# Three transformer layers and a rotation on one core: the set-up reordered, clears moved to GpSimd

## The reference

```
mod = silu(cond) @ W_ada + b_ada           # shift, scale, gate, twice
h = layernorm(x) * (1 + scale1) + shift1
q, k, v = split(h @ W_qkv + b_qkv)          # 16 heads of 9
x = x + gate1 * (softmax(q k^T / 3) v @ W_proj + b_proj)
h = layernorm(x) * (1 + scale2) + shift2
x = x + gate2 * mlp(h)                      # 576 wide, gelu; layer 1: 4 experts, top 2
```

## Time and profile before

| | |
|---|---|
| median of 3 runs | 1291.34 us (1290.72 to 1295.43) |
| the profiled execution | 1287.96 us, of which span 1285.8 us |
| busy: PE, DVE, ACT, POOL | 1196.0, 908.0, 783.2, 744.0 us |
| chain that ended last | PE 79%, DVE 14%, issue 3%, ACT 1%, DMA 1% |
| PE busy in the 40 slices of 32 us | first slice 2 tenths, second 8, then 9 nearly throughout |
| granted PE clock in the same slices | 9, 6, 8 tenths, then mostly 9 |

### The profile page before, as it was taken

One profiled execution on the slowest core, in us unless ns is written; L12 is line 12 of the kernel. 1 busy time (PEld: TensorE's weight loads), 2 busy tenths in 40 slices (PEclk: granted clock), 3 DMA queues, 4 the chain that ended last, 5 costly groups with the idle time before them and its releaser, 6 DMA issues.

```text
span 1285.8 us, 35560 instructions
## 1 busy us (share of the span) xinstructions
PE 1196.0 (93%) x12842; PEld 957.8 (74%) x12842; DVE 908.0 (71%) x2505; ACT 783.2 (61%) x1801; POOL 744.0 (58%) x2221
## 2 busy tenths in 40 slices
PE   2899999989989999999998999999979999999997
PEld 1577777768767677778887888888767777777775
DVE  6689999866489999965664654646479999964432
ACT  2489888756479888962331432332468898864531
POOL 3665656566566665566667666677777777700000
PEclk9689999899989999999998999999979999989997
DMA  6322122332351112221110110110021111001120
GB/s 169 61 13 21 17 22 18 47 90 32 53 128 17 20 16 20 21 56 5 14 15 4 16 15 4 17 51 19 17 52 31 34 34 27 20 6 19 20 65 28
DMA packets 50320, 42.83 MB, mean 33 GB/s; under 512 B 8455, under 2 KB 45754, under 8 KB 49717
## 3 DMA queue, kind: packets, MB, share of 16 engines
q1 hardware_dynamic: 45884, 29.91, 10.4%
q0 software_dynamic: 3488, 8.52, 8.3%
q10 hardware_dynamic: 780, 2.17, 0.5%
HBM read 33.86 MB, written 3.03 MB: 29 GB/s over the span
## 4 chain that ended last, share of the span: by engine, by line
PE 79%; DVE 14%; issue 3%; ACT 1%; DMA 1%; SPq 0%; DVEq 0%; ACTq 0%
PE PS L1659 17%; PE PSA L1383 14%; PE PS L1464 7%; PE PSA L1440 7%; PE PS L1425 7%; PE PS L1383 6%; DVE BIG L547 3%; PE PS L1495 2%; PE PSB L1635 2%; PE PS L1485 2%; PE PS L1496 2%; PE PSB L1447 1%; PE PS L1490 1%; PE PS L1475 1%; PE PSB L1383 1%
## 5 line engine op out<-in xcount | busy, mean ns | idle before, releaser
L1245 ACT ACTIVATE BIG<-PSA 128x512 f32<-128x512 f32 (+1 forms) x224 | 132.0, 593 | 279.0 <-PE PSA L1383 278.8
L1659 PE MATMUL PS<-w,BIG 128*128 128x144 f32 (+1 forms) x1920 | 257.6, 289 | 9.7 <-DVE BIG L811 6.5
L1659 PEld LDWEIGHTS PS<-w,BIG 128*128 128x128 f32 (+1 forms) x1920 | 247.5, 191 | 18.1 <-DVE BIG L811 7.8
L547 DVE TENSOR_REDUCE BIG<-PSA 128x8 f32<-128x1024 f32 x192 | 234.2, 1220 | 33.2 <-PE PSA L1440 31.7
L1114 ACT ACTIVATE BIG<-PSB 128x1024 f32<-128x1024 f32 x192 | 195.6, 1019 | 19.6 <-PE PSB L1447 19.5
L1440 PEld LDWEIGHTS PSA<-KK,Q 32*128 32x128 f32 x1536 | 109.0, 195 | 63.3 <-issue 41.2
L1440 PE MATMUL PSA<-KK,Q 32*128 32x128 f32 x1536 | 134.0, 292 | 21.1 <-DVE BIG L547 10.7
L1425 PE MATMUL PS<-K,qt 128*128 128x128 f32 x768 | 125.0, 289 | 11.1 <-DVE qt L542 5.4
L1447 PE MATMUL PSB<-Q,KK 32*128 32x128 f32 x1536 | 133.3, 292 | 0.0
L1464 PE MATMUL PS<-BIG,VA 128*32 128x128 f32 x3072 | 127.6, 285 | 1.1 <-DVE col L422 1.1
L1856 POOL MEMSET qprod<- 128x2 f32 x63 | 6.3, 100 | 201.5 <-DMA VB<-QA 201.5
(11 more groups left out here) (302 smaller groups left out, 2977.6 us busy)
## 6 DMA issues: line engine op xcount, KB each, us to landing
gate<-gates SPq DMA_DIRECT2D x96, 72.0 KB, 2.9
mgate<-gates SPq DMA_DIRECT2D x96, 72.0 KB, 2.8
VB<-skew POOLq DMA_DIRECT2D x16, 288.0 KB, 3.7
X<-in_x SPq DMA_DIRECT2D x4, 576.0 KB, 14.0
out<-X SPq DMA_DIRECT2D x8, 288.0 KB, 3.6
BIG<-in_skew_w SPq DMA_DIRECT2D x2, 1024.0 KB
w<-in_w SPq DMA_DIRECT2D x1, 1440.0 KB, 11.4
BIG<-in_wqkv SPq DMA_DIRECT2D x2, 584.0 KB
```

The source lines that it names most:

```text
L547: V.tensor_reduce(nmax.rearrange("p (s w) -> p s w", w=HP)[:, 2 * a:2 * a + 2, 3 * HD:3 * HD + G], PSA[:, :].rearrange("p (r g k) -> p r g ...
L1245: S.activation(hm[0:rows, slot, :], PS[(par * FTOT[l] + j) % 2][0:rows, :], gelu).then_inc(gelu_done, 1)
L1659: last = mm(o, hm[0:rows, slot, s * 128:(s + 1) * 128], w2[0:rows, FT * e + k, :], start=(k == 0), stop=(k == FT - 1))
```

## The change

Five edits, all in the set-up:

1. SP: the first quarter of `x` is issued ahead of layer 0's column weights, not behind them.
2. ACT: the copies of the column products and of `QA` (with the waits that they need) come ahead of the issues of the gate weights and of the column weights of layers 1 and 2.
3. DVE gives the clears of `h3`, `qt` and `VA` and their ones to POOL, which does them between its constants and its first broadcast. The semaphores follow: `h3_set` (DVE waits for it before its first low part), `qt_set`, `va_zero` (ACT and PE).
4. DVE: `constant_parts` comes first, ahead of the first statistics.
5. DVE: the second quarter's statistics are taken inside `pair(-1)`, after `h_second(0)`, not before it.

```diff
 # sync
+            load_x(0)
             sp.dma_start(AC0[0], d["ada_col"][0:C0, 0:AC]).then_inc(ld_ada0, 16)
             load_rows(sp, AC1[0], d["ada_col"][:, 0:AC], ld_ada0)
...
-            for q in range(4):
+            for q in range(1, 4):
                 load_x(q)
 # vector
-            V.memset(h3[:, :, :].bitcast(F32), 0.0)
-            V.memset(qt[:, :, :, :, :].bitcast(F32), 0.0).then_inc(qt_set, 1)
-            dve.wait_ge(qt_set, 1)
-            for g in range(G):
-                last = V.memset(qt[:, :, 1, HG * g:HG * g + HG, 3 * HD + g:3 * HD + g + 1].bitcast(F32), 1.0)
-            last.then_inc(qt_set, 1)
...
-                def pair(i, dev=None):
+                def pair(i, dev=None, stats=None):
...
                     if 0 <= i + 1 < NL:
                         h_second(i + 1)
+                    if stats:
+                        first_stats(stats)
                     step(1)
...
                 if l == 0:
+                    constant_parts()
                     first_stats(0)
                     columns(0, PS[1])
                     deviations(0, 0, 0)
                     pair(-2)
                     qkv_split(0)
-                    values_clear(1)
-                    constant_parts()
-                    first_stats(1)
-                    pair(-1)
+                    dve.wait_ge(h3_set, 1)
+                    pair(-1, stats=1)
 # scalar: the nine issues of ada_gate and of ada_col for l in (1, 2) go from
 # ahead of act.wait_ge(s_const, 2) to behind the copy of QA
...
-                        act.wait_ge(va_set, (1, 1, 3)[l])
+                        act.wait_ge(va_zero, 1) if l < 2 else act.wait_ge(va_set, 2)
 # tensor
-                        pe.wait_ge(va_set, 2 + 2 * (l // 2))
+                        pe.wait_ge(va_zero, 2)
+                        pe.wait_ge(va_set, 1 if l < 2 else 3)
 # gpsimd, behind the tensor_scalar that writes UT
+            R.memset(h3[:, :, :].bitcast(F32), 0.0).then_inc(h3_set, 1)
+            R.memset(qt[:, :, :, :, :].bitcast(F32), 0.0).then_inc(qt_set, 1)
+            R.memset(VA[:, :, :, :], 0.0).then_inc(va_zero, 1)
+            pool.wait_ge(qt_set, 1)
+            for g in range(G):
+                last = R.memset(qt[:, :, 1, HG * g:HG * g + HG, 3 * HD + g:3 * HD + g + 1].bitcast(F32), 1.0)
+            last.then_inc(qt_set, 1)
+            pool.wait_ge(va_zero, 1)
+            for j in range(2):
+                at = j * (HD + 1) + HD
+                last = R.memset(VA[:, :, 8 * j:8 * j + 8, at:at + 1], 1.0)
+            last.then_inc(va_zero, 1)
```

More of the change, by code:

```diff
@@ L181, in program @@
         qkv_ps, qk_hi, qk_lo, v_ev, va_set = (sem("qkv_product"), sem("qk_high"), sem("qk_low"), sem("v_ready"), sem("va_set"))
+        h3_set, va_zero = sem("h3_set"), sem("values_cleared")
         qk_turn, qk_rd, qk_dup, qt_set = sem("qk_turned"), sem("qk_ready"), sem("qk_doubled"), sem("qt_set")
@@ L270, in _ @@
             sp.dma_start(K[:, :], d["consts"]).then_inc(ld_cond, 16)
-            sp.dma_start(AC0[0], d["ada_col"][0:C0, 0:AC]).then_inc(ld_ada0, 16)
-            load_rows(sp, AC1[0], d["ada_col"][:, 0:AC], ld_ada0)
             def load_x(q):
@@ L277, in load_x @@
                              d["x"][q * 8:(q + 1) * 8].rearrange("b t c -> t b c")).then_inc(ld_x[q], 16)
+            load_x(0)
+            sp.dma_start(AC0[0], d["ada_col"][0:C0, 0:AC]).then_inc(ld_ada0, 16)
+            load_rows(sp, AC1[0], d["ada_col"][:, 0:AC], ld_ada0)
             def load_raw(name, n, s):
@@ L405, in constant_parts, with values_clear @@
                 V.memset(oq[:, :, C:C + 1], 1.0).then_inc(va_set, 1)
-            def values_clear(n):
+            def values_clear():
                 V.memset(VA[:, :, :, :], 0.0).then_inc(va_set, 1)
-                dve.wait_ge(va_set, n)
+                dve.wait_ge(va_set, 2)
                 for j in range(2):
@@ L879, in mlp_step @@
                     if m == 6:
-                        values_clear(3)
+                        values_clear()
                     if not last:
@@ L1008, in _ @@
                 load_rows(act, wr3[k * C1:(k + 1) * C1, :], d["wqkv0"], ld_wq)
[L1009 to L1012, removed]
-                load_rows(act, AC1[l], d["ada_col"][:, l * AC:(l + 1) * AC], ld_ada)
             act.wait_ge(s_const, 2)
@@ L1022, in _ @@
             S.activation(QA[:, :], PS[6][:, 0:C], ACT.Copy).then_inc(q_at, 1)
+            act.dma_start(AG0, d["ada_gate"][0:C0, :]).then_inc(ld_gw, 16)
+            load_rows(act, AG1, d["ada_gate"], ld_gw)
+            for l in (1, 2):
+                act.dma_start(AC0[l], d["ada_col"][0:C0, l * AC:(l + 1) * AC]).then_inc(ld_ada, 16)
+                load_rows(act, AC1[l], d["ada_col"][:, l * AC:(l + 1) * AC], ld_ada)
             def mlp_cast(l, q):
```

## The result

The changed kernel took 1275.32 us (median of 4 executions, 1265.83 to 1281.95). The kernel before took 1291.03 us beside it (4 executions, 1289.20 to 1295.43). The ratio on record is 0.9891, 95% interval 0.9848 to 0.9935; it is not the quotient of the two medians, which is 0.9878. Its profiled execution took 1275.29 us (span 1273.0); the one of before took 1287.96 (span 1285.8). The later experiments, with more executions of both kernels, put the difference at 6 to 7 us of the mean: 1286.2 for the kernel before (85 later executions), and 1279.5 for the changed one (28, the first four among them) or 1280.3 (24, without them). Three of all these executions, each over 1.5% above the fastest of its kernel, are left out of the ratios and kept in the means.

A forecast was written before the change was run, and what follows sets the result against it. It took the set-up chain (x's transfer, then DVE's unbroken work until PE's first qkv product at 27.98 us) as the bound; 2.9 + 2.45 + 0.5 = 5.85, say 5.8, off the 1291.34 median gave 1285.5, range 1280.0 to 1291.0.

The forecast's parts named there:

- medians move by a few us: Whole time: the scatter allowed for medians when judging the chance of being faster by over 0.5%, put at 0.44.
- Part 1: Set-up loads: first quarter of x ahead, columns later; columns copied at 12.7 instead of 15.62, gain 2.9 us.
- they start at 6.0 and share: SP's queue: column weights start at 6.0 us beside ACT's qkv weights, landing taken as 9.9.
- A: Column weights land late, 10.45 us after issue, at 13.0; gain only 2.8 us, time 1288.5; chance 0.12.
- B: Column weights take 15.1 us, landing at 17.7; loss of 1.9 us, time 1293.2; chance 0.05.
- Part 2: DVE: nothing left between the weights' split and the low parts, which wait for ACT's high parts; gain 2.45 us.
- Part 3: Clears on POOL: 5120 columns, over between 9.0 and 16.0 us, taken as 10.5; cost 0.
- Part 4: DVE's steps after the columns run before POOL's first two-input instruction; gain 0.5 us, from 0 to 0.9.
- POOL's clears read no data and stand beside DVE's idle time: Set-up: the reason why DVE's gain from a quiet POOL could not go below 0.
- Rival C: PE's clock helps: denser start changes one pair, 3.6 us more, 1281.9; against it, PE's row-maximum wait remains; chance 0.15.
- D: PE's clock hurts: one pair more at the low level, 3.6 us lost, time 1289.1; chance 0.09.
- E: Does nothing: another engine takes the gain back before the end, time 1291; chance 0.03.

The follow-up runs named there:

- loads' order: Kernel before with only the first quarter of x issued ahead of the column weights: 1283.49 us, ratio 0.9992.
- ACT's copies: Kernel before with only ACT's copies moved ahead of its nine later issues: 1279.83 us, ratio 0.9991.
- clears, statistics: Changed kernel with the load order and ACT's copies taken back, leaving clears on POOL, constants first, statistics moved: 1286.2 us, ratio 1.0024.
- changed, delayed: Changed kernel with five further clears of MW3 on DVE ahead of the first low part: 1285.4 us, ratio 0.9978.
- before, clock kept up: Kernel before with 104 added identity products on PE, placed in its three waits: 1294.07 us, ratio 1.0043.
- wait away: Changed kernel with MW3's clear and the last sixteen statistics moved into DVE's idle time inside pair(-1): 1274.62 us, ratio 0.9892; repeated, 1276.49 us, 0.9924.
- wait away, clock kept up: Changed kernel with MW3's clear and last sixteen statistics inside pair(-1), plus 26 identity products in PE's three waits: 1273.51 us, ratio 0.9919.
- better version: Changed kernel with MW3's clear and last sixteen statistics inside pair(-1), and POOL's clears held until silu is done: 1271.83 us, ratio 0.9868.
- the pair of traces above: Two repeat runs of the changed kernel, no edit: 1281.69 us, ratio 0.9936, and 1281.81 us, ratio 0.9942; their traces' spans were 1280.7 and 1268.8 us.
- the third trace of the same kernel: Changed kernel run a third time, no edit, against the kernel before: 1281.81 us, ratio 0.9942.

## Why the prediction missed

Two steps failed. In the sum, it is the load order, 1.2 us short. In the time, it is "medians move by a few us": the sum goes from the 1291.34 of before to a median of the changed kernel as if only the set-up lay between them, and puts the scatter of executions at nothing in the forecast and at a few us in the range. The runs showed a gain of 7.54 us at the product, 6 to 7 at the end, and executions of one and the same kernel 20 us apart, which is where the rest of the 16 is most likely from.

**All executions together.** Call lost clock (1 - the mean granted clock) times the span. Over 195 executions of these kernels, a level for each kernel plus one slope leaves a scatter of 3.3 us. The slope is 0.47 us for each microsecond lost (0.43 within the kernel before alone). The earlier trace rows say the same: a pair at the low level takes 3.6 us more and loses 7.9 (half of 15.8), which is 0.46. The kernel before lost 17.9 to 55.6 us of clock in its executions and took 1275.7 to 1295.7.

| kernel | product | executions, mean | at no lost clock, against before |
|---|---|---|---|
| before | 27.98 | 85, 1286.2 | 0 |
| loads' order | 23.38 | 10, 1281.8 | -5.2 |
| ACT's copies | 25.89 | 10, 1280.2 | -2.7 |
| clears, statistics | 24.38 | 10, 1284.8 | -2.0 |
| changed | 20.07 to 20.44 | 28, 1279.5 | -6.4 |
| changed, delayed | 30.42 | 12, 1285.9 | +2.1 |
| before, clock kept up | 35.95 | 12, 1293.5 | +4.4 |
| wait away | 20.28, 20.70 | 15, 1275.5 | -8.9 |
| wait away, clock kept up | 19.68 | 6, 1274.3 | -13.9 |
| better version | 20.60 | 6, 1271.6 | -10.6 |

A value of 10 executions is good to about 1 us (one standard error). The last column follows the first, roughly: 7.5 us at the product are 6.4 at the end, and 2.4 us of delay are 2.1. It has a weakness that the pair of traces above shows: before the first recorded fall the record says 1.00 whatever PE's level is, so a kernel that rises and falls early has a loss on record that a kernel low from the start has not. This flatters the kernel with the wait away and the clock kept up: its mean is 1.2 us below that of the kernel without the added products, and this column says 5.0. The executions ran on three chips; the kernel before, at no lost clock, stands within 1.6 us on all of them.

Where the clock is lost is much the same in every trace: in all fourteen of them the recorded clock falls between 340 and 380 us, between 900 and 960, and in the last 40 us. No edit here touches those stretches.

**Part 1, the load order: right in kind, 1.2 us short, for a wrong reason.** The failed step is "they start at 6.0 and share". The working took ACT's delay for SP's queue: q1's first bytes moved about 1 us after the first issue (0.74 and 1.75), not 1.9, and x and the weights were through on q1 before ACT's q10, with its first issue at 4.20, moved a byte. `x` landed at 6.7 (issued at 2.13, and 4.6 more; forecast 7.5) and PE started on the weights at 8.63, not 9.9: just below the 8.8 that I had called undisturbed. The columns were copied 4.09 earlier instead of 2.9. The statistics, forecast "near 7.5", started at 9.29, because DVE was still at silu and the constant parts; they were over 0.46 us before the columns came, so this cost nothing. Rivals A and B, on late weights, fell: 5.9 us from their first issue to the last landing (2.61 to 8.49), not 10.45 or 15.1. (B's break-even, given as a landing at 16.1, is 15.8 by the working's own terms.)
**Part 2, nothing before the low parts: right.** PE's turn to the low parts took 5.88 and takes 3.51: 2.37, forecast 2.45. ACT released them, and the statistics were hidden.

**Part 3, clears on POOL: right at the fast end.** 0.9 ns a column and over at 9.4 with the small ones (forecast 10.5); PE had no wait for `U`.

**Part 4, DVE beside POOL: the gain was there, its lower bound was wrong.** From the columns' copy to PE's turn of the first pair took 5.40 and takes 4.47: 0.93 (forecast 0.5, and 0.9 was the upper end), as POOL's first two-input instruction came only at 17.54. But "POOL's clears read no data and stand beside DVE's idle time" failed: they hit DVE's silu, 2.77 us for 0.18, and the column products were released by DVE in three traces (8.21 with edits 3 to 5 alone, 8.32 in two of the changed kernel). The single run with the clears held back shows the cause, and no cost in the changed kernel: there the weights release PE at 8.58, no earlier, and the product is at 20.32. The Trainium skill ("SBUF — State Buffer", Who interferes with whom) has the hit side: a `tensor_scalar` in its fast mode contends with GpSimd for the shared port pair, and whoever issued first holds it. The trace agrees that DVE was held: its step began at 4.57 and ended at 7.34, as the second clear did (7.30), while the third ran from 7.25. It does not settle who came first (the first clear started at 4.62), nor why DVE waited for two clears and not one; and no view shows the mode of the step. The other half of the section, which the prediction had used, now has its row too: a `tensor_tensor` of DVE at 7.98 took 0.19 us beside the third clear, as it did in the kernel before.

**The sum.** 4.09 + 0.93 + 2.37 = 7.39 of the 7.54 us seen at the product, and 0.15 between the low parts and the product (1.08 and 0.93), against a forecast of 5.85 and an upper end of 7.3.

**The clock: why 16 and not 7.** In the pair of profiled executions the spans differ by 12.8 us, 5.3 more than at the product, and that is clock: 0.976 against 0.966 is 30.6 us lost against 43.7, and 13.1 x 0.47 = 6.2. Rival C had against it that "that wait remains". It stood at 0.39 us, so C is what this pair shows, and its price was too small: the lead grew from 7.5 to 13.9 us by 91.67, 6.4 for the 3.6 that one pair was given, as PE was low from 44.6 to about 75 before, and only up to 45 after. But C as a mechanism of the change fell too: the third trace of the same kernel has the wait, 3.42 us, and the low level behind it, and over all executions the changed kernel lost as much clock on record as before (37.6 against 38.4 us). D, the opposite, fell by the same numbers, and E, that another engine takes the gain back, by the table.

What the working had put at nothing is luck in the two medians. The four executions of before lay at 1289 to 1295, in the upper third of a distribution 20 us wide, and their mean is 5.5 us above that of the 85; the changed kernel's four lay 6 us below its later 24. The working went by the profiled execution plus 3.4 to reach the median of before. Drawing four and four of the later executions at random gives a median difference of 5.6 +- 4.6 us, and 15.7 or more in 2% of draws. So the likeliest reading is 6 to 7 us of set-up and 9 of luck. It is a reading: that the 16 did not come back in two repetitions is shown, and that nothing else differed in the first comparison (on which chip it ran is not on record) is not. That each single gain was invisible in its ratio has the same cause.

**What stays open.** Why the level rises at 30 us in one execution, at 45 in another and at 54 in a third of the same program; two of these traces show PE's work at the same times up to 28.3 us. Why the later falls, such as the one at 1120, differ from execution to execution. Whether the better version loses less clock because of its missing wait (29.8 us against 37.6) or by luck: 6 executions don't settle it, its own trace fell at 37 without the wait, and the kernel with only the wait removed lost 34.5 in 15. Its edge at equal clock over the changed kernel, 4.2 us, is about three times its uncertainty (1.5).

## What to carry to other kernels

In a set-up, follow the chain of waits to the first main product and price each link; here 7.5 us there were 6 to 7 at the end, and the two loads that SP issued first were through before ACT's queue had moved a byte. When executions of one kernel differ by 20 us, take the time from many of them before explaining a difference of 16, and find in the traces where two executions part: here most of it was 1100 us behind the place that had been changed. And look for work of an engine that others wait for soon, lying ahead of a result: moving 5.4 us of DVE's work into its idle time gave 2.5 us more here (8.9 against 6.4, with a standard error of 1.1), and PE's second row of scores came 2.3 us earlier in the trace.

## What the runs showed of the hardware

- Two back-to-back clears on GpSimd (0.94 and 1.79 us) stretched a 32-column `tensor_scalar` of DVE from 0.18 to 2.77 us: it ended as the second did. With the clears behind it, 0.18 again. A `tensor_tensor` beside the next clear kept its 0.19.
- A GpSimd clear of 2048 float32 columns takes 1.79 to 1.85 us, as fast as on DVE (1.78).
- The granted clock on record is 1.00 until its first recorded change, even where PE works at the low level: the first score products took 1.11 us for eight at a recorded 1.00, and 0.66 at the high level. So 1.00 and 0.50 stood on record for the same work at the same level (44 to 52 us, the two traces of one kernel). At the start of a trace the matmuls' own durations tell the level, not the record.
- Each microsecond of granted clock lost on record cost 0.47 us in this kernel, and the same program lost from 18 to 56 us of it from one execution to the next.
